# Cross-attention on one core: the turned output of an older superstep moves to the end of TensorE's superstep, and its accumulation one superstep later

## The reference, cut to what matters

```python
qp = q @ wi;  kp = k @ wi;  vp = v @ wi          # k = v = ctx (25088 x 512), q = layernorm(x) (256 x 512), wi 512 x 64
scores = einsum('bsd,btd->bst', qp, kp) / sqrt(64)
attn = softmax(scores, axis=-1)
head = qp + einsum('bst,btd->bsd', attn, vp)
x = x + tile(head, 16) @ Wo + bo
...                                               # attention block and experts follow, from x
```

## Time and profile before

| | us |
|---|---|
| median of 3 runs | 541.46 |
| lowest, highest | 540.64, 542.77 |
| profiled execution, its span | 538.8 |
| cross-attention in it | 0 to about 222 |

### The profile page before, as it was taken

One profiled execution on the slowest core, in us unless ns is written; L12 is line 12 of the kernel. 1 busy time (PEld: TensorE's weight loads), 2 busy tenths in 40 slices (PEclk: granted clock), 3 DMA queues, 4 the chain that ended last, 5 costly groups with the idle time before them and its releaser, 6 DMA issues.

```text
span 538.8 us, 11302 instructions
## 1 busy us (share of the span) xinstructions
PE 506.0 (94%) x4322; PEld 349.0 (65%) x4322; DVE 418.4 (78%) x703; ACT 330.0 (61%) x645; POOL 37.5 (7%) x116
## 2 busy tenths in 40 slices
PE   5889999999999999889998999899799999999995
PEld 2434544454454547669766777687688888888875
DVE  2378777777877788778475876998898998999994
ACT  2644554554456463656474647877578778778772
POOL 4000111101110000000312000000000000000000
PEclk9999999999999999999999999999899999999998
DMA  8969989888986800246320403559787997895001
GB/s 325 349 252 386 397 323 347 326 319 320 381 321 231 311 2 4 75 192 221 139 79 9 150 0 153 188 220 335 278 297 274 364 348 252 337 360 185 1 0 43
DMA packets 35939, 122.48 MB, mean 227 GB/s; under 512 B 2609, under 2 KB 2609, under 8 KB 31282
## 3 DMA queue, kind: packets, MB, share of 16 engines
q1 hardware_dynamic: 35602, 121.27, 60.7%
q10 hardware_dynamic: 288, 0.52, 0.3%
HBM read 121.26 MB, written 0.52 MB: 226 GB/s over the span
## 4 chain that ended last, share of the span: by engine, by line
PE 73%; DVE 13%; ACT 5%; issue 3%; DVEq 0%; POOL 0%; ACTq 0%
PE score_banks L1214 14%; PE bank L529 13%; PE bank L1250 7%; PE score_banks L561 7%; PE bank L576 6%; PE score_banks L808 2%; DVE w_split L1898 2%; PE bank L545 2%; DVE w_split L2042 2%; PE score_banks L991 2%; ACT xprobs L1296 1%; PE bank L770 1%; PE score_banks L1015 1%; PE score_banks L1138 1%; PE bank L1223 1%
## 5 line engine op out<-in xcount | busy, mean ns | idle before, releaser
L1296 ACT ACTIVATE xprobs<-score_banks,small 128x512 f32<-128x512 f32 (+1 forms) x104 | 67.8, 663 | 88.4 <-DVEq L1761 75.3
L1898 DVE TENSOR_TENSOR w_split<-arena,w_split 128x1024 fp32r<-128x1024 f32 x96 | 113.7, 1219 | 5.9 <-ACT w_split L1451 4.2
L1451 ACT ACTIVATE w_split<-arena 128x1024 fp32r<-128x1024 f32 x96 | 100.6, 1060 | 13.9 <-PE score_banks L1214 8.9
L529 PE MATMUL bank<-arena,wi_sb 128*64 128x512 f32 (+1 forms) x400 | 91.4, 598 | 6.2 <-DMA arena<-in_ctxT 6.2
L1214 PE MATMUL score_banks<-w_split,xg 128*128 128x512 f32 x384 | 89.1, 390 | 0.0
L1770 DVE STREAM_TRANSPOSE xprobsT<-xprobs 128x1024 f32<-128x1024 f32 (+1 forms) x52 | 61.4, 1183 | 33.2 <-ACT xprobs L1296 32.1
L1214 PEld LDWEIGHTS score_banks<-w_split,xg 128*128 128x128 f32 x384 | 71.6, 188 | 16.1 <-DVE w_split L1898 0.7
L1742 DVE TENSOR_REDUCE small<-score_banks 128x2 f32<-128x1024 f32 (+1 forms) x52 | 57.4, 1142 | 12.2 <-PE score_banks L561 12.1
L529 PEld LDWEIGHTS bank<-arena,wi_sb 128*64 128x64 f32 x400 | 26.8, 138 | 55.1 <-issue 54.1
L561 PE MATMUL score_banks<-k_full,hT 64*32 64x256 f32 (+1 forms) x1664 | 49.0, 367 | 2.7 <-ACT xprobs L1296 2.6
L1250 PE MATMUL bank<-w_split,hidT 128*128 128x512 f32 x168 | 41.1, 401 | 0.9 <-DVE hidT L2205 0.9
(11 more groups left out here) (361 smaller groups left out, 764.2 us busy)
## 6 DMA issues: line engine op xcount, KB each, us to landing
arena<-in_ctxT SPq DMA_DIRECT2D x24, 2048.0 KB, 8.6
arena<-in_w12T SPq DMA_DIRECT2D x32, 1024.0 KB, 5.6
arena<-in_w3T SPq DMA_DIRECT2D x16, 1024.0 KB, 6.0
arena<-in_fKT SPq DMA_DIRECT2D x4, 1024.0 KB, 7.3
arena<-in_fV SPq DMA_DIRECT2D x4, 1024.0 KB, 5.3
arena<-in_Wo SPq DMA_DIRECT2D x1, 2048.0 KB
arena<-in_ctxT SPq DMA_DIRECT2D x4, 256.0 KB, 4.9
arena<-in_kKT SPq DMA_DIRECT2D x1, 1024.0 KB, 11.7
```

Of the source, the lines that this page charges most:

```text
L529: last = pe.matmul(kp_bank[p][DH * h:DH * (h + 1), 0:half], wi_sb[:, k, :], tokens[:, h * half:(h + 1) * half], start=(k == 0), stop=(k == ...
L1296: act.activation(xprobs[:, qb, 0:2 * width].rearrange("p (h n) -> p h n", h=2), score_banks[:, 2 * p:2 * p + 2, 256 * q:256 * q + width], ...
L1451: act.activation(w_split[:, i % 4, 0, :], raw, ACT.Copy).then_inc(part_high, 1)
L1898: return dve.tensor_tensor(w_split[:, i % 4, 1, :], raw, w_split[:, i % 4, 0, :].bitcast(F32), ALU.subtract)
```

## The change

`turn_o(u - 2)` leaves its place between `scores(u, 0)` and `next_keys(u + 1, 0)` and stands behind `pv(u - 1, 1)`, in front of `turn_keys(u + 1, ...)`. VectorE takes the turned output one superstep later: `add_o(u - 3)` stands where `add_o(u - 2)` stood, with the fade of the other parity. The first such copy is made in superstep 3 instead of 2. `add_o(LAST - 4)`, which was in superstep `LAST - 2`, comes into the written-out superstep `LAST - 1`, right behind `chunk_max(LAST - 1, 1, 0)`. From `add_o(LAST - 3)` on the order is as it was. No instruction is added or left out.

```diff
             def superstep(u, par):
                 scores(u, par, 0)
-                if not isinstance(u, int) or u >= 2:
-                    turn_o(u - 2)
                 next_keys(u + 1, 0)
                 pv(u - 1, 1 - par, 0)
                 scores(u, par, 1)
                 next_keys(u + 1, 1)
                 pv(u - 1, 1 - par, 1)
+                turn_o(u - 2)
                 turn_keys(u + 1, 1 - par, 0)
                 turn_keys(u + 1, 1 - par, 1)
...
             pe.matmul(kp_bank[0], fold[:], wo_sum, start=True, stop=True).then_inc(ev("wo_folded"), 1)
-            turn_o(LAST - 4)
             pv(LAST - 3, 1, 0)
             pe.wait_ge(ev("wo_dup_ready"), 2)
             next_keys(LAST - 1, 0)
             scores(LAST - 2, 0, 1)
             next_keys(LAST - 1, 1)
             pv(LAST - 3, 1, 1)
+            turn_o(LAST - 4)
             turn_keys(LAST - 1, 1, 0)
             turn_keys(LAST - 1, 1, 1)
...
-            def superstep(u, b, first_o=False):
+            def superstep(u, b, take_o=True, first_o=False):
                 chunk_max(u, b, 0)
-                add_o(u - 2, b, first=first_o)
+                if take_o:
+                    add_o(u - 3, 1 - b, first=first_o)
                 turn_probs(u, b, 0)
...
-            superstep(2, 0, first_o=True)
-            superstep(3, 1)
+            superstep(2, 0, take_o=False)
+            superstep(3, 1, first_o=True)
...
             chunk_max(LAST - 1, 1, 0)
+            add_o(LAST - 4, 0)
             for st in range(ST):
```

## The result

| | before | after |
|---|---|---|
| median of 7 runs each, us | 542.15 | 545.31 |
| lowest, highest | 540.64, 542.77 | 543.5, 548.26 |
| ratio, 95% interval | | 1.0071 (1.0052 to 1.009) |
| profiled execution, span | 538.8 | 543.6 |
| mean granted clock of it | 0.994 | 0.991 |

By the ratio, which is taken over all runs, the change makes the kernel slower by 0.7%, some 3.9 us (the two medians are 3.2 us apart), where 1.95 were forecast. The time lies outside the range that was given, 541.0 to 545.0.

The account below looks back on a forecast made before the run. The prediction took VectorE's softmax ring with ScalarE to bound the loop and TensorE its end. It added 0 for the loop and 1.95 us for the wait to 541.46, giving 543.4 us, range 541.0 to 545.0.

Parts of the forecast that it names:

- The loop: Nine supersteps, `u` = 2 to 10: effect taken as 0, between -1.0 and +2.3 us, period staying at 15.8 us.
- VectorE's ring: In the loop, maximum, exponentials (ScalarE), transposes, next maximum: period 15.76 us, in which nothing waits for TensorE.
- TensorE's gain of 0.1 us: Loop: `turn_o` takes 0.26 instead of 0.37 us in its new place, 0.11 us less TensorE work per superstep.
- The wait: Superstep 11: `turn_o(LAST - 3)` waits for `add_o(LAST - 4)`, TensorE going on at 189.36 instead of 187.41, +1.95 us.
- a few hundredths: Superstep 11: semaphore time from the end of `add_o` at 189.30 until TensorE goes on at 189.36.
- the lead of 0.7 us: Loop, superstep 6: TensorE about 0.7 us ahead of VectorE's need; 0.26 us of added work comes out of it.
- Nothing behind the wait took the delay up: After superstep 11: all that follows comes 1.95 us later; the rival, wait hidden between 193 and 205, had chance 0.08.
- TensorE's clock falls in the new wait: Rival, superstep 11: at half the clock `pv(10)` takes 3.6 us more, 547.0 us in all; chance 0.03.
- a stretch with 0.49 us of work in 2 us: Profile row cited against the clock rival: the granted clock stayed at 1.00, the level of 2.4 GHz, there.

Follow-up runs that it names:

- loop_alone: Changed kernel with `turn_o(LAST - 3)` moved behind `pv(LAST - 2)` and `add_o(LAST - 3)` behind `turn_probs`, so the wait is gone and the new loop stays: 542.54 us, ratio 1.0002.
- wait_alone: Kernel before with its old loop, only `add_o(LAST - 4)` moved into superstep `LAST - 1` behind the maximum, so `turn_o(LAST - 3)` waits for it: 545.23 us, ratio 1.007.
- two_fills: Kernel before with 15 instead of 8 useless matmuls at the softmax's end and 14 more in the idle time at 382: 539.62 us, ratio 0.9961.
- after_again: The changed kernel, unaltered, run and profiled again: 546.27 us against 541.61 for the kernel before, ratio 1.0078.
- before_look: The kernel before, unaltered, run for one more profile: 542.03 us.

## Why the prediction was wrong

**The loop: right.** 0 was taken between -1.0 and +2.3, and loop_alone measures +0.02% with an interval of 0.17%, or 0.9 us, either way. The reasons hold in the rows: VectorE's ring has no idle time for TensorE, and TensorE's gain of 0.1 us goes into a wait for the exponentials (2.01 us against 1.88).

**The wait: right in place and mechanism, a little small.** 1.95 us were summed, with 1.7 to 2.3 as bounds. wait_alone has 2.03, the whole change 2.27. The first 0.08 us lie in the step from `add_o` to TensorE, for which the sum had 0.06 us ("a few hundredths") and no row; in wait_alone `turn_o` starts at 188.73, which is 0.14 us after the end of `add_o` (187.98 + 0.61):

```profile
187.98 0.61 DVE L1788 SCALAR_TENSOR_TENSOR o_acc<-o_acc,small,bank 128x128 f32<-128x128 f32 x2 [0.26 <-DVE small L1759]
```

The other 0.24 us are the lead of TensorE that was given up in the loop: the reduce of superstep 11 idles 0.23 us for scores, which it did not before, so `add_o(LAST - 4)` starts that much later. The sum took the lead of 0.7 us from superstep 6; in superstep 11 of the kernel before, the reduce at 184.91 stands 1.21 us behind the start of its scores, so there nothing of the lead was left:

```profile
183.70 1.96 PE L561 MATMUL score_banks<-k_full,hT 64*32 64x256 f32 x64
```

Nothing behind the wait took the delay up, as said. In runs of equal mean clock the change costs 2.29 us, which is this term.

**The failing step: the rival "TensorE's clock falls in the new wait".** It was given a chance of 0.03 because a stretch with 0.49 us of work in 2 us had kept a clock of 1.00, and so the sum had no term for the clock. That row was one execution, and right behind the row's own place the clock falls in five other profiles (223.47, 225.20 twice, 221.79, 221.32). The same profile also held a counter-example: at 385.89 the clock falls where TensorE had been busy for 1.00 of the 3.89 us ahead of it (the rows under two_fills). With the whole wait in the kernel, the fall comes behind it in four of six profiles. Its price was over-stated at 3.6 us: in after_again `pv(10)` lost 1.68 us (5.29 against 3.61). The outcome is the prediction plus that rival, not one or the other.

Yet the rival, as it was put, holds only about half of what was lost to the clock. An estimate from these few profiles: falls behind the wait, 4/6 x 1.68 = 1.1 us; falls near 222, (4/5 - 1/6) x 1.66 = 1.05 us, at a place to which the prediction gave no price and no chance. (At 363.77 to 368.57, three of six against two of eight tell no difference.) The mean clocks bear out the sum of the two: over the 13 timed runs of the changed kernel the mean clock is 0.9874, so (1 - 0.9874) x 544 = 6.9 us of granted clock are missing, against (1 - 0.991) x 541.6 = 4.9 us before; 2.0 us more, and with the delay of 2.27 us that makes 4.3, against 3.9 and 4.2 measured.

A hint was there ahead of the result, in the kernel's own runs: the same program took 540.64 and 542.77 us, farther apart than the whole forecast effect, and a single profile shows only one execution of it.

The Trainium skill, "TensorE: Matmul & The Clock Gate", section "HAM oscillation", names idle time between bursts as what brings the lower level, in a kernel whose waits are longer than this one. The runs agree, and show it for 1.85 us: filling the idle time raises the mean clock (0.986 to 0.993 at the wait in the changed kernel, 0.991 to 0.997 with two_fills), while a busy delay of the same length does not lower it. They also show a fall without an idle time ahead of it (363.77 in before_look).

**What stays open.** Why the fall near 222 comes more often when there is an idle wait 30 us ahead of it (four of five profiles against one of six) was not found. Nor what brings the fall at 363.77 to 368.57, ahead of which TensorE was busy. Nor why the same idle wait is followed by a fall in some executions and not in others. Nor why the two kernels with a busy delay have fewer falls than the kernel before (0.993 and 0.992 against 0.991): the delay moves everything behind it by 2 us, but that this matters was not tried by itself.

## What to carry to other kernels

A new wait of TensorE has two prices: its length, which can be read from the rows ahead of time, and a fall of the clock behind it, which comes in some executions only and can cost as much again. So one profile with a granted clock of 1.00 over an idle time is no proof; look at the spread of the runs and at their mean clock. Where a wait can't be taken away, matmuls of no use in it are worth a try, and for this change the cheap way is to move the consumer: behind `pv`, `turn_o` waits for nothing (loop_alone). That takes the loss away, and leaves no gain over the kernel before.

## What the runs showed of the hardware that was not expected

The same program gives several times that follow its mean granted clock in steps: the kernel before takes 540.4 us at 0.994, 541.9 at 0.991 and 543.1 at 0.988 (means of 4, 9 and 7 runs of one comparison). Each fall seen in the middle of a profile lasts 3.41 us or, once, 6.83 us, at 0.50. An idle time of 1.85 us was followed by one in four of six profiles, one of 1.5 us at the end of the softmax in five of eleven, and one of 3.1 us (382 in the kernel before) in all thirteen profiles where it was not filled.
